# A graph layer's edge sums on one core: buckets that begin at any chunk, with the last pair of chunks shared by two buckets

## What is computed

```
agg = segment_sum(x[src], dst);  z = relu(((1 + eps) * x + agg) @ W1 + b1) @ W2 + b2
z   = batchnorm(z) * gamma + beta + x
x1  = layernorm(x + z)
y   = relu(segment_sum(edge_weight[:, None] * x1[dst], src) @ weight)
out = layernorm(x1 + y)
```

## Time and profile before

| | us |
|---|---|
| median of three runs | 4302.68 |
| the three runs | 4298.88 to 4304.92 |
| the profiled execution | 4298.99 |
| its span, first to last instruction | 4297.1 |
| busy PE / POOL / DVE / ACT | 3404.5 / 3201.3 / 2603.3 / 414.1 |

### The profile page before, as it was taken

The page is one execution under the profiler, slowest core; times in us unless marked ns, Lnnn a source line. Parts: engine busy times, 40 slices in busy tenths (PEclk is TensorE's granted clock), DMA queues, the critical chain, the costliest instruction groups (busy, mean ns, idle before and its releaser), DMA issues.

```text
span 4297.1 us, 69357 instructions
## 1 busy us (share of the span) xinstructions
PE 3404.5 (79%) x16119; PEld 2813.5 (65%) x16120; DVE 2603.3 (61%) x5756; ACT 414.1 (10%) x1049; POOL 3201.3 (74%) x3456
## 2 busy tenths in 40 slices
PE   3877887877878788778737988888888888888887
PEld 3766666666766676667636766676666676666666
DVE  5887877877888788787475443443434434444343
ACT  0000000000000000000152000000000000000001
POOL 7777777777777777777647777777777777777775
PEclk7988988998989898898858999999999999999998
DMA  8444444444444444444594334344343443434433
GB/s 274 117 119 116 121 119 115 121 119 116 121 118 119 115 121 119 119 119 118 168 327 149 115 115 120 115 120 118 116 120 115 120 119 116 120 115 120 120 115 99
DMA packets 271185, 553.04 MB, mean 129 GB/s; under 512 B 85374, under 2 KB 147742, under 8 KB 271128
## 3 DMA queue, kind: packets, MB, share of 16 engines
q0 software_dynamic: 159424, 434.52, 35.1%
q10 hardware_dynamic: 62724, 70.85, 5.0%
q1 hardware_dynamic: 48980, 46.98, 3.4%
HBM read 489.80 MB, written 59.72 MB: 128 GB/s over the span
## 4 chain that ended last, share of the span: by engine, by line
POOL 64%; issue 22%; PE 6%; DMA 3%; SPq 2%; POOLq 1%; ACT 1%; DVE 1%; ACTq 0%; DVEq 0%
POOL ring L575 33%; POOL ring L643 31%; PE ps L1580 2%; PE ps L1363 2%; DMA x_dram<-ring 1%; SPq L464 1%; PE ps L1446 1%; POOLq L677 1%; ACT ring L1815 1%; POOL ring L581 0%; DMA ring<-in_x,idx 0%; DMA z_dram<-z_pair 0%; DMA ring<-x_dram,idx 0%; DMA ring<-in_x 0%; POOLq L678 0%
## 5 line engine op out<-in xcount | busy, mean ns | idle before, releaser
L575 POOL DMA_INDIRECT ring<-in_x,idx x1664 | 1591.5, 956 | 495.2 <-issue 473.1
L643 POOL DMA_INDIRECT ring<-x_dram,idx x1612 | 1525.9, 947 | 499.9 <-issue 495.4
L1580 PE MATMUL ps<-ring,work 128*128 x6448 | 1518.5, 391 | 304.7 <-SPq L542 300.1
L1580 PEld LDWEIGHTS ps<-ring,work 128*128 128x128 f32 x6448 | 1221.9, 194 | 585.7 <-issue 425.6
L1233 DVE TENSOR_SCALAR work<-ps,dstT,wT 128x256 f32<-128x256 f32 x1612 | 741.5, 533 | 1092.0 <-PE ps L1580 1029.2
L1363 PE MATMUL ps<-ring,ones_sb 128*128 x3324 | 915.2, 424 | 350.6 <-SPq L479 316.6
L1363 PEld LDWEIGHTS ps<-ring,ones_sb 128*128 128x128 f32 x3324 | 680.3, 212 | 502.3 <-issue 401.7
L1446 PEld LDWEIGHTS ps<-work 128*128 128x128 f32 x3384 | 430.9, 197 | 15.2 <-DVE work L936 0.3
L1446 PE MATMUL ps<-work 128*128 128x128 f32 x3384 | 429.3, 279 | 0.0
L951 DVE SCALAR_TENSOR_TENSOR ones_sb<-ps,tile_base,dstT 128x256 f32<-128x256 f32 (+1 forms) x294 | 311.6, 1099 | 67.1 <-PE ps L1346 30.5
L931 DVE TENSOR_TENSOR work<-ps,current 128x768 f32<-128x768 f32 x282 | 266.3, 944 | 16.5 <-PE ps L1446 16.5
(11 more groups left out here) (250 smaller groups left out, 2122.9 us busy)
## 6 DMA issues: line engine op xcount, KB each, us to landing
ring<-in_x,idx POOLq DMA_INDIRECT x1664
ring<-x_dram,idx POOLq DMA_INDIRECT x1612, 2.7
z_dram<-z_pair ACTq DMA_DIRECT2D x49, 256.0 KB, 2.7
ones_sb<-x_dram ACTq DMA_DIRECT2D x49, 256.0 KB, 3.7
x_dram<-zero_row SPq DMA_DIRECT2D x24, 512.0 KB, 8.9
ring<-z_dram SPq DMA_DIRECT2D x24, 512.0 KB, 6.2
ring<-in_x SPq DMA_DIRECT2D x24, 512.0 KB, 7.2
x_dram<-ring ACTq DMA_DIRECT2D x24, 512.0 KB, 5.0
```

The costliest lines, as they stand in the source:

```text
L575: nc.gpsimd.indirect_dma_start(out=ring[:, q, c, :], out_offset=None, in_=x, in_offset=bass.IndirectOffsetOnAxis(ap=idx[:, q, c:c + 1], ax ...
L643: nc.gpsimd.indirect_dma_start(out=ring[:, q, c, :], out_offset=None, in_=x1_dram, in_offset=bass.IndirectOffsetOnAxis(ap=idx[:, q, c:c + ...
L1580: last = nc.tensor.matmul(to[:, t * D:(t + 1) * D], ones_of[:, b, c, t * P:(t + 1) * P], ring[:, ds((p + b) & (RING - 1), 1), c, :].rearra ...
```

## The change

Buckets now begin at any chunk. `chunks_i` counts a bucket's chunks, at least one, rounded up to 128 edges, and a bucket's first chunk is the sum of the chunks before it. A pair belongs to the bucket of its first chunk. A bucket's first pair is (first chunk + 1) >> 1, its end is (chunks to its end + 1) >> 1, and ODD2 says whether the last pair's second chunk belongs to the following bucket.

The last pair of a bucket always stands alone (`border2`, from BODY2 = end - 1); the others are summed as before. PE now clears the following bucket's bank after the last head group and the single pair, ahead of the border pair, and one clearing matmul stands before the first bucket. For the border pair it waits for the landing and the one-hot matrix, then sums the second chunk into the following bank where ODD2 is set, or into its own where it isn't, and then the first chunk into its own.

DVE has one more tile of one-hots, `border2`. `table2` gets two columns more (BODY2, ODD2); DVE and PE read seven values of it.

```diff
         chunk_at_i = sb("chunk_at_i", [P, BLOCKS], i32)
         chunk_row = sb("chunk_row", [P, BLOCKS], f32)
         chunk_row_i = sb("chunk_row_i", [P, BLOCKS], i32)
-        pairs_i = sb("pairs_i", [P, NB1], i32)
+        chunks_i = sb("chunks_i", [P, NB1], i32)
+        ends_i = sb("ends_i", [1, 3, NB1], i32)
         first_chunk = sb("first_chunk", [P, NB1], f32)
-        pairs_to = sb("pairs_to", [P, NB1], f32)
-        first_pair = sb("first_pair", [P, NB1], f32)
-        batches_i = sb("batches_i", [1, 3, NBK], i32)
+        chunks_to = sb("chunks_to", [P, NB1], f32)
+        first_pair = sb("first_pair", [1, NB1], f32)
+        body_to = sb("body_to", [1, 2, NBK], f32)
+        batches_i = sb("batches_i", [1, 4, NBK], i32)
         rounds_i = sb("rounds_i", [1, 2], i32)
-        table2 = sb("table2", [1, NBK, 6], mybir.dt.uint16)
+        table2 = sb("table2", [1, NBK, 8], mybir.dt.uint16)
         work = sb("work", [P, WORK], f32)
         zero_row = sb("zero_row", [P, D], f32)
         all_ones = work[:, 3200:3200 + P]
...
         p_sumT = ps[:, 2:4, :]
         p_conv = ps[:, 4:6, :]
         at_ones = 2 * BW * D
-        ones2 = work[:, at_ones:at_ones + (ALONE + 1) * 2 * BUCKET].rearrange("p (b c n) -> p b c n", c=2, n=BUCKET)
+        ones2 = work[:, at_ones:at_ones + (ALONE + 2) * 2 * BUCKET].rearrange("p (b c n) -> p b c n", c=2, n=BUCKET)
         loop2 = ones2[:, 0:2 * TWO]
         heads2 = ones2[:, 2 * TWO:ALONE]
         last2 = ones2[:, ALONE:ALONE + 1]
-        assert at_ones + (ALONE + 1) * 2 * BUCKET <= 8704 and 8704 + KH * D <= WORK
+        border2 = ones2[:, ALONE + 1:ALONE + 2]
+        assert at_ones + (ALONE + 2) * 2 * BUCKET <= 8704 and 8704 + KH * D <= WORK
         x1_bucket = ones_flat[:, 0:8 * BW * D].rearrange("p (i t d) -> p i t d", t=BW, d=D)
         diagonal = ones_flat[:, 8 * BW * D:8 * BW * D + 2 * BW * P].rearrange("p (b t n) -> p b t n", b=2, t=BW)
         summed2 = work[:, 0:BW * D].rearrange("p (t d) -> p t d", t=BW)
...
                 skip_runtime_bounds_check_because=IN_RANGE)
             return values
 
-        def entry2(eng, j):
+        def entry2(eng, j, columns):
 
             _, values = nc.values_load_multi_w_load_instructions(
-                table2[0:1, ds(j, 1), :].rearrange("a t f -> a (t f)"), engines=[eng.engine], min_val=0, max_val=ROWS,
+                table2[0:1, ds(j, 1), columns].rearrange("a t f -> a (t f)"), engines=[eng.engine], min_val=0, max_val=ROWS,
                 skip_runtime_bounds_check_because=IN_RANGE2)
             return values
 
...
 
 
         SHARED, NEW, HEAD, M4, M2, OFF, SWEEP, END, LOW, REP = range(10)
-        NEW2, M42, HEAD2, M22, END2, PREV2 = range(6)
+        PREV2, NEW2, M42, HEAD2, M22, BODY2, END2, ODD2 = range(8)
         MOST = max(ROUNDS * NT, PADP, TILE_ONES * NT)
         assert MOST < 1 << 16
 
...
 
                 after(NS, 0)
                 setup(nc.vector.tensor_scalar(region_i[:, :], filled[:, :], float(2 * SLOTS + PAIR - 1), None, ALU.add))
-                setup(nc.vector.tensor_scalar(pairs_i[:, :], filled[:, :], float(PAIR - 1), None, ALU.add))
+                setup(nc.vector.tensor_scalar(chunks_i[:, :], filled[:, :], 1.0, float(P - 1), ALU.max, ALU.add))
                 sync()
                 setup(nc.vector.tensor_scalar(region_i[:, :], region_i[:, :], 8, None, ALU.arith_shift_right))
-                setup(nc.vector.tensor_scalar(pairs_i[:, :], pairs_i[:, :], 8, None, ALU.arith_shift_right))
+                setup(nc.vector.tensor_scalar(chunks_i[:, :], chunks_i[:, :], 7, None, ALU.arith_shift_right))
                 sync()
                 setup(nc.vector.tensor_tensor_scan(runs_to[:, :], many[:, :], region_i[:, :], 0.0, ALU.mult, ALU.add))
-                setup(nc.vector.tensor_tensor_scan(pairs_to[:, :], many[:, :], pairs_i[:, :], 0.0, ALU.mult, ALU.add))
+                setup(nc.vector.tensor_tensor_scan(chunks_to[:, :], many[:, :], chunks_i[:, :], 0.0, ALU.mult, ALU.add))
                 sync()
                 setup(nc.vector.tensor_tensor(begin_row[:, :], runs_to[:, :], region_i[:, :], ALU.subtract))
-                setup(nc.vector.tensor_tensor(first_pair[:, :], pairs_to[:, :], pairs_i[:, :], ALU.subtract))
+                setup(nc.vector.tensor_tensor(first_chunk[:, :], chunks_to[:, :], chunks_i[:, :], ALU.subtract))
                 sync()
                 setup(nc.vector.tensor_scalar(begin_row[:, :], begin_row[:, :], 2.0, 2.0, ALU.mult, ALU.add))
-                setup(nc.vector.tensor_scalar(first_chunk[:, :], first_pair[:, :], 2.0, None, ALU.mult))
                 sync()
 
             def run_targets():
...
             def chunk_rows():
 
                 setup(nc.vector.tensor_tensor(shifted[:, 1:NB1 + 1], begin_row[:, :], first_chunk[:, :], ALU.subtract))
+                setup(nc.vector.tensor_scalar(ends_i[:, 0, :], first_chunk[0:1, :], 1.0, None, ALU.add))
+                setup(nc.vector.tensor_scalar(ends_i[:, 1, :], chunks_to[0:1, :], 1.0, None, ALU.add))
+                setup(nc.vector.tensor_copy(ends_i[:, 2, :], chunks_to[0:1, :]))
+                sync()
+                setup(nc.vector.tensor_tensor(jump[:, :], shifted[:, 1:NB1 + 1], shifted[:, 0:NB1], ALU.subtract))
+                setup(nc.vector.tensor_scalar(ends_i[:, 0:2, :], ends_i[:, 0:2, :], 1, None, ALU.arith_shift_right))
+                setup(nc.vector.tensor_scalar(ends_i[:, 2, :], ends_i[:, 2, :], 1, None, ALU.bitwise_and))
+                sync()
+                setup(nc.vector.tensor_tensor(taken[0:1, 0:NBK], ends_i[:, 1, 0:NBK], ends_i[:, 0, 0:NBK], ALU.subtract))
+                setup(nc.vector.tensor_copy(first_pair[:, :], ends_i[:, 0, :]))
+                setup(nc.vector.tensor_copy(table2[0:1, :, END2], ends_i[:, 1, 0:NBK]))
+                setup(nc.vector.tensor_copy(table2[0:1, :, ODD2], ends_i[:, 2, 0:NBK]))
+                sync()
+                setup(nc.vector.tensor_scalar(batches_i[:, 3, :], taken[0:1, 0:NBK], -1.0, 0.0, ALU.add, ALU.max))
                 setup(nc.vector.tensor_scalar(rounds_i[:, 0:1], first_pair[0:1, NBK:NB1], float(RING - 1), float(2 * RING), ALU.add, ALU.max))
                 setup(nc.vector.tensor_copy(rounds_i[:, 1:2], first_pair[0:1, NBK:NB1]))
-                setup(nc.vector.tensor_scalar(batches_i[:, 0, :], pairs_i[0:1, 0:NBK], 1, None, ALU.arith_shift_right))
                 setup(nc.vector.tensor_copy(table2[0:1, :, NEW2], first_pair[0:1, 0:NBK]))
-                setup(nc.vector.tensor_copy(table2[0:1, :, END2], pairs_to[0:1, 0:NBK]))
                 sync()
-                setup(nc.vector.tensor_tensor(jump[:, :], shifted[:, 1:NB1 + 1], shifted[:, 0:NB1], ALU.subtract))
+                setup(nc.vector.tensor_scalar(batches_i[:, 0, :], batches_i[:, 3, :], 1, None, ALU.arith_shift_right))
+                setup(nc.vector.tensor_tensor(body_to[:, 0, :], first_pair[0:1, 0:NBK], batches_i[:, 3, :], ALU.add))
                 setup(nc.vector.tensor_scalar(rounds_i[:, 0:1], rounds_i[:, 0:1], 5, None, ALU.arith_shift_right))
+                sync()
+                setup(nc.vector.tensor_copy(table2[0:1, :, BODY2], body_to[:, 0, :]))
                 setup(nc.vector.tensor_scalar(chosen[0:1, 0:NBK], batches_i[:, 0, :], 2.0, float(BATCH), ALU.mult, ALU.min))
-                setup(nc.vector.scalar_tensor_tensor(out=pairs_to[0:1, 0:NBK], in0=batches_i[:, 0, :], scalar=2.0, in1=first_pair[0:1, 0:NBK],
+                setup(nc.vector.scalar_tensor_tensor(out=body_to[:, 1, :], in0=batches_i[:, 0, :], scalar=2.0, in1=first_pair[0:1, 0:NBK],
                                                      op0=ALU.mult, op1=ALU.add))
                 sync()
                 setup(nc.vector.scalar_tensor_tensor(out=batches_i[:, 1, :], in0=batches_i[:, 0, :], scalar=2.0, in1=chosen[0:1, 0:NBK],
                                                      op0=ALU.mult, op1=ALU.subtract))
-                setup(nc.vector.tensor_tensor(first_pair[0:1, 0:NBK], pairs_to[0:1, 0:NBK], chosen[0:1, 0:NBK], ALU.subtract))
+                setup(nc.vector.tensor_tensor(first_pair[0:1, 0:NBK], body_to[:, 1, :], chosen[0:1, 0:NBK], ALU.subtract))
                 sync()
                 setup(nc.vector.tensor_scalar(batches_i[:, 2, :], batches_i[:, 1, :], TWO, None, ALU.bitwise_and))
                 setup(nc.vector.tensor_copy(table2[0:1, :, HEAD2], first_pair[0:1, 0:NBK]))
...
                     sync()
                 setup(nc.vector.tensor_tensor(chunk_row_i[:, :], chunk_row[:, :], chunk_at[:, :], ALU.add))
                 sync()
-                nc.vector.tensor_copy(table2[0:1, :, M22], pairs_to[0:1, 0:NBK]).then_inc(s_chunks, 1)
+                nc.vector.tensor_copy(table2[0:1, :, M22], body_to[:, 1, :]).then_inc(s_chunks, 1)
 
             def regions_and_targets():
                 bucket_regions()
...
                                                in1=ps[:, 2 + n % 2, 0:size], op0=ALU.mult, op1=ALU.add).then_inc(s_keys2, 1)
 
             def steps2(j):
```

(35 more changed lines are left out.)

## The result

The changed kernel takes 4273.5 us, median of five runs (4271.23 to 4283.15), beside 4303.92 for the kernel before (4298.88 to 4305.15). The ratio is 0.9933, with a 95% interval of 0.9922 to 0.9944: 0.67% faster, 30.4 us by the medians. The profiled execution took 4271.23 us with a span of 4268.5, 28.6 us less than the span before.

A forecast was written before the change was run, and what follows sets the result against it. POOL's even gather pace was taken to bound the second stage, with PE following. Gathers 30.0 us plus the end's net 1.5 make 31.5 us off the median 4302.68: 4271 us, with an 8 in 10 range of 4261 to 4284.

The forecast's parts named there:

- The gathers: Second stage on POOL: 1588 gathers instead of 1612, 24 fewer at 1.2518 us, 30.0 us saved, all on the path.
- The tables: Building the second stage's tables on DVE grows by 1.4 to 1.8 us, costing nothing, with 20 us of cover.
- a sign that something reached the path: Sign of being wrong: a moved first gather would mean the tables' 1.4 to 1.8 us or the new layout mattered.
- The end: After the stage's last gather: 1.8 us less for one pair, 0.3 us more for control, net 1.5 us saved.
- The term for control: Two more conditions on PE between the last landing and the first matmul, taken at 0.3 us.
- one pair is left in place of two, 1.8 us less: After the last landing PE sums one pair instead of two, saving half of 3.55 us, 1.8 us.
- The number: The forecast time of the whole changed kernel: 4271 us, from the median 4302.68 less 31.5; chance 84%.
- PE's reserve: Second stage: PE needs 31.17 us for a bucket of 16 pairs, POOL 40.1, leaving PE 8.9 us of slack.
- the rival's deciding point: The slower rival decides the time from 40.5 us a bucket on PE, 9.0 us above now.
- The slower rival: PE's control becomes the second stage's bound through skipped conditional bodies, 43.7 us a bucket, 4460 us in all; chance 4%.
- the DVE work queued behind the weighting: Normalisation of buckets three and four back, 1.9 us late at worst, needed only by the output product a bucket later.
- The rule of the Trainium skill: A taken branch whose target isn't in the pages at hand stalls for a fetch, putting every skipped border body at risk.

The follow-up runs named there:

- the kernel with even chunks: The changed kernel with each bucket's chunks rounded up to an even number, restoring 806 pairs and 1612 gathers: 4294.44 us, ratio 1.0000 to the kernel before.
- the two loads: The changed kernel with 20 or 60 unused matmuls of zeros more in each bucket: 4375.18 and 5145.53 us, where the kernel before takes 4294.72.
- the moved waits: The changed kernel with the border pair's two waits moved behind the two conditions on whose bucket the second chunk is: 4266.89 us in one run.

## Why the prediction was right

**The gathers: right.** 1588 of them, as counted from the inputs, 946 ns each, no wait for PE. At 1.2502 us 24 are 30.0 us, the term of the sum. The stretch shrank by 32.6; the other 2.5 us are 1587 times the 1.6 ns by which the pace of that run of before lay above the changed kernel's, and above the 1.2501 of the kernel with even chunks. That kernel shows that nothing but the pairs is in the gain, and the waits that of these it is the gathers.

**The tables: right.** They took from 2107.17 to 2111.48, 4.3 us in place of 2.2, so 2.1 more where I had 1.4 to 1.8, and DVE then stood until 2135.37 waiting for ACT. The first gather of the stage came 3.2 us later, which I had named as a sign that something reached the path. It was none: with the same tables it stands at 2248.3 and 2245.6 with the two loads and 2249.9 with the moved waits, and at 2248.0 with even chunks, whose tables take a step more, on both sides of the 2249.2 of before, if on another chip. And the kernel with even chunks, which has the new tables, takes the time of the kernel before on its chip. In the changed kernel's run POOL's last list write, ahead of any use of the table of rows, already began at 2223.84 in place of 2219.02; why isn't shown.

**The end: wrong in size and sign,** +0.8 us in place of -1.5. The term for control was right, 0.33 us measured and 0.3 taken. The step that failed is "one pair is left in place of two, 1.8 us less". The pair is one, but it cost 3.35 us instead of 1.8, at a clock of 0.56 behind 2.68 us of standing still. I had priced it at the clock of a busy stretch. Of the idle time 1.72 us stood there before; the 0.96 more are 0.51 of later landing, for which the sum had no term, 0.33 of conditions, and 0.1 of what PE had to do ahead of it. Whether the clock falls behind such a wait can't be told from its length. In the same trace eleven waits of 2.29 to 2.60 us for landings lie inside the stage, and over the 3.5 us behind them the clock was 1.00 four times and 0.53 to 0.66 seven times. The longest but one of them, of 2.58 us, kept it:

```profile
3645.54 7.44 PE L1601 MATMUL ps<-ring,work 128*128 x32 [2.58 <-SPq L545]
...
3645.50:3652.90 7.40, 7.35 (x32) 5.91 (x32) 7.40 (x18) 0.00 (x0) 5.57 (x7) 1.00 0.37 109
```

So a longer idle time made the slow pair likelier, and in both traces of this end on undisturbed chips, with 2.68 and 2.35 us, it came; in the kernel with even chunks, with 2.02 us, it didn't. That it must come with the change isn't shown.

**The number.** 4271 against 4273.5 is off by 2.5 us, and the end's 2.3 us would fill that; but the runs of the changed kernel spread over 12 us. In the two profiled runs two things that weren't forecast nearly cancel, the first gather 3.2 us later and the pace of before 2.5 us slower than usual. Neither comes from the change as far as the runs show, so that is luck.

**PE's reserve: wrong, without harm.** "All of it costs nothing while it stays under 8.9 us a bucket", and the rival's deciding point 9.0 us above now, were read from a stretch in which PE was late but only in its first buckets, when no earlier bucket had been added up by DVE yet. The bucket from 2353.77 in the earlier trace rows is the third, so its output product had nothing to wait for. Under 4.7 us of load PE became the bound. Control as such was free, as forecast: the changed kernel's clearing matmuls in that stretch stand 31.17 us apart, as before's do.

```profile
2355.17 0.38 PE L1589 MATMUL ps<-zeros 1*128 1x512 bf16 x1
2355.49 1.99 PE L1626 MATMUL ps<-ring,work 128*128 x8
2357.32 1.03 PE L1640 MATMUL ps<-ones_sb 128*128 128x256 f32 x4
2358.18 13.98 PE L1601 MATMUL ps<-ring,work 128*128 x64
...
2386.34 0.38 PE L1589 MATMUL ps<-zeros 1*128 1x512 bf16 x1
```

The slower rival had the right engine and the wrong mechanism (and a slip in its sum: 31.17 and 12.2 are 43.4 us a bucket, not 43.7, which makes some 4445 of its 4460): what would make PE the bound is not skipped code but DVE's addition with eight pairs of cover where it had ten, and the clock that fell behind that wait. The prediction called the DVE work queued behind the weighting harmless because the output product needs it a bucket later. It needs it in the same bucket, behind the first head group. The rule of the Trainium skill (Runtime: NRT & Kernel Launch, Instruction fetch mechanics) on taken branches had no price in this stretch: 31.17 us on both sides, with the border bodies and their conditions added on one.

## What to carry to other kernels

Where one queue paces a stage at an even step, the value of a change is the number of its steps that go, counted from the data, and an experiment that keeps the new order but restores the old count shows whether anything else is in it. Don't read an engine's reserve from the stretch in which it catches up at the beginning: ask first which waits on other engines aren't there yet, and load the engine on purpose to find the edge. Work after the last arrival should be priced at both levels of TensorE's clock, as a range, and not at the one of the busy stretch before: behind some 2.5 us of waiting either came. And before reading a pace as the price of one engine's step, check on that chip which engine waits for which.

## What the runs showed of the hardware

TensorE's granted clock behind idle time went with its length, but not by it alone. At the ends of the stage it was 1.00 behind 1.72 and 2.02 us of standing still, and 0.56 and 0.63 behind 2.68 and 2.35. Inside the stage it was 1.00 behind four and 0.53 to 0.66 behind seven of the changed kernel's eleven waits of 2.29 to 2.60 us, and still 1.00 behind one of 2.71 us in the kernel with even chunks. Under 20 small matmuls a bucket it fell behind all 33 waits of 2.28 us or more and behind four of 13 of 1.41 to 1.77. At the lower level two pairs take 6.4 in place of 3.6 us.

An indirect gather of a chunk of padding, whose 128 rows should all be one, landed 3.64 to 3.98 us after its start in twelve places inside the stage of before, where the median of all steps is 2.74, and 3.52 and 3.57 at the end; where two such gathers end the stage, the last landed after 4.08 and 4.24 us. That it is the equal rows is likely; no run varied them alone.

A gather's own duration on POOL stayed at 945 to 948 ns in the mean on all chips, even where gathers stood 1.50 us apart. There PE was late and stood up to 20.3 us ahead of a weight load without a cause that the profile shows, and POOL stood too: from 3000 to 5200 us in the changed kernel 105.1 us for PE's sums by name, and 286.6 us, up to 7.9 at a time, for a releaser that the profile doesn't know. What slows those chips stays open.

```profile
PEld ps L1601 <- issue: 492.7, 229, 20.3
...
POOL ring L646 <- remote: 286.6, 95, 7.9
...
POOL ring L646 <- PE ps L1601: 105.1, 55, 4.0
```
